# Three landing slots of three cells, transposed tiles in halves, and a stripe's left cells loaded ahead of its far cells

## The reference

```python
h = jnp.maximum(_layernorm(x, axis=-1), 0.0)
A_hat = adj + jnp.eye(adj.shape[0], dtype=adj.dtype)
d_inv_sqrt = jnp.sum(A_hat, axis=1) ** (-0.5)
A_norm = d_inv_sqrt[:, None] * A_hat * d_inv_sqrt[None, :]
support = h @ W.T
return x + jax.nn.relu(A_norm @ support)
```

## Time and profile before

| | us |
|---|---|
| median of 3 runs | 1440.7 |
| lowest, highest | 1440.1, 1442.88 |
| the profiled execution | 1437.75 |
| its span, first to last instruction | 1436.0 |

### The profile page before, as it was taken

One profiled execution on the slowest core, in us unless ns is written; L12 is line 12 of the kernel. 1 busy time (PEld: TensorE's weight loads), 2 busy tenths in 40 slices (PEclk: granted clock), 3 DMA queues, 4 the chain that ended last, 5 costly groups with the idle time before them and its releaser, 6 DMA issues.

```text
span 1436.0 us, 8302 instructions
## 1 busy us (share of the span) xinstructions
PE 1020.2 (71%) x2363; PEld 458.5 (32%) x2363; DVE 810.7 (56%) x692; ACT 511.0 (36%) x1390; POOL 52.6 (4%) x61
## 2 busy tenths in 40 slices
PE   1441354566867758759598889798899799889673
PEld 1430122222323323324243334333344234334231
DVE  5342235265656557667578677676666356556342
ACT  2685566456447354262524162524000000000001
POOL 4000000000000000000000000000000100000001
PEclk9765586787988889889899989999999899999886
DMA  9869999999998989899677796969799999898952
GB/s 308 278 250 340 322 343 324 333 310 345 341 310 264 354 222 283 262 248 297 206 248 190 221 277 179 284 184 256 212 265 272 252 272 260 266 269 219 262 118 59
DMA packets 253885, 377.07 MB, mean 263 GB/s; under 512 B 10000, under 2 KB 178064, under 8 KB 253840
## 3 DMA queue, kind: packets, MB, share of 16 engines
q1 hardware_dynamic: 136208, 192.50, 46.5%
q10 hardware_dynamic: 117632, 184.04, 41.9%
HBM read 372.31 MB, written 4.19 MB: 262 GB/s over the span
## 4 chain that ended last, share of the span: by engine, by line
DMA 36%; PE 28%; DVE 13%; ACT 11%; ACTq 4%; SPq 3%; issue 3%; POOL 0%; POOLq 0%; DVEq 0%
DMA slot<-in_adj_dram 36%; PE bank L441 27%; DVE adjT L631 9%; ACT slot L485 8%; DVE part L619 3%; ACT junk L496 3%; ACTq L289 2%; ACTq L252 1%; SPq L300 1%; SPq L307 1%; ACT acc L471 1%; SPq L315 1%; DMA out_dram<-near 1%; SPq L252 0%; ACTq L260 0%
## 5 line engine op out<-in xcount | busy, mean ns | idle before, releaser
L441 PE MATMUL bank<-adjT,support 128*128 128x512 f32 x2048 | 974.6, 636 | 309.6 <-DVE adjT L631 309.4
L631 DVE STREAM_TRANSPOSE adjT<-slot 128x2048 f32<-128x2048 f32 x211 | 483.6, 2303 | 410.4 <-DMA slot<-in_adj_dram 276.5
L441 PEld LDWEIGHTS bank<-adjT,support 128*128 128x128 f32 x2048 | 411.2, 205 | 851.6 <-issue 489.4
L496 ACT ACTIVATE junk<-slot 128x384 bf16<-128x384 f32 (+3 forms) x396 | 214.9, 544 | 307.2 <-issue 195.6
L485 ACT ACTIVATE slot<-slot 128x6656 f32<-128x6656 f32 (+12 forms) x52 | 165.4, 3183 | 90.7 <-issue 51.0
L514 ACT ACTIVATE near<-near,dinv 128x128 f32<-128x128 f32 x64 | 20.5, 390 | 408.3 <-DVE near L714 408.3
L496 ACT ACTIVATE junk<-near 128x256 bf16<-128x256 f32 (+1 forms) x176 | 69.3, 394 | 79.2 <-issue 72.4
L631 DVE STREAM_TRANSPOSE adjT<-near 128x2048 f32<-128x2048 f32 x31 | 71.2, 2300 | 38.7 <-PE bank L441 38.7
L619 DVE TENSOR_REDUCE part<-slot 128x5 f32<-128x1920 f32 (+3 forms) x36 | 84.0, 2334 | 0.0
L496 ACT ACTIVATION_READ_ACCUMULATOR junk<-slot 128x1 f32 x396 | 74.0, 187 | 0.0
L376 POOL TENSOR_TENSOR dinv<-total,power 128x4 f32<-128x4 f32 x16 | 16.1, 1008 | 895.8 <-DVE total L675 895.8
(11 more groups left out here) (53 smaller groups left out, 182.7 us busy)
## 6 DMA issues: line engine op xcount, KB each, us to landing
slot<-in_adj_dram SPq DMA_DIRECT2D x58, 1024.0 KB, 12.6
slot<-in_adj_dram ACTq DMA_DIRECT2D x58, 1024.0 KB, 15.6
slot<-in_adj_dram SPq DMA_DIRECT2D x66, 768.0 KB, 11.2
slot<-in_adj_dram ACTq DMA_DIRECT2D x66, 768.0 KB, 12.0
near<-in_adj_dram SPq DMA_DIRECT2D x30, 512.0 KB, 15.5
near<-in_adj_dram ACTq DMA_DIRECT2D x30, 512.0 KB, 16.7
third<-in_adj_dram SPq DMA_DIRECT2D x28, 256.0 KB, 15.6
third<-in_adj_dram ACTq DMA_DIRECT2D x28, 256.0 KB, 14.9
```

Of the source, the lines that this page charges most:

```text
L441: ins = nc.tensor.matmul(bank[g % BANKS][:], support[:, v * R + r, :], adjT[n % TURNS][:, r, :], start=(n == first_of[g] and r == 0), stop ...
L496: nc.scalar.activation(junk[at % JUNKS][:, :n], cells[:, c, :], ACT.Copy, accum_out=part[u % 2][:, k, c:c + 1]).then_inc(junk_done, 1)
L631: nc.vector.transpose(adjT[n % TURNS][:].rearrange("p t (c i) -> p t c i", i=Q), cells.rearrange("p c (t r) -> p t c r", r=Q)).then_inc(t_ ...
```

## The change

The numbers: slots of 3 cells, three of them (72 KB a partition in place of 64); `adjT` is a tile of half a cell, three of them (12 KB in place of 16); a cell is transposed in two instructions of 1024 elements, and its product waits for each half by itself. In the second pass the three `third` tiles, one tensor now, are a fourth slot, free once column 15 has been transposed. Small tensors of the start (stats, w_sb, wT, ones_at and others) move into `acc`, whose rows are unused by then. Pieces: 118 in place of 96 (45 left in place of 36, 38 far in place of 32, 35 again in place of 28), and 432 DMAs of them in place of 360. Of left and again pieces 53 have three cells, 25 two and two one; before 27 had four, 31 three, four two and two one.

Order: a stripe's left pieces are loaded first, then far, then near and third. `FIRST` left cells go ahead of the column in every stripe. ACT still issues two landings ahead (`AHEAD = 2`), but each now waits for the landing three before it. SP's list has the same waits and no other bound. Stripe 0 has 13 far cells, more than the 12 that a slot holds in its far form, so it gets a fifth piece of one cell's width, a second column set in `far_sum`, and one addition on VectorE. In the second pass the stores and ACT's relu stand by a rule of places: ahead of the load whose slot's former piece is transposed later than the result is combined.

```diff
-    MOST = 4
-    SLOTS = 2
-    TURNS = 2
+    MOST = 3
+    SLOTS = 3
+    AHEAD = 2
+    HALVES = 2
+    TURNS = 3
...
     for u in range(NB):
-        cells = NB - 1 - u - BAND
-        far[u] = []
-        per = 0 if cells <= 0 else min(B, MOST * C // (B * cells))
-        for b0 in range(0, B if per else 0, per or 1):
-            far[u].append(len(landing))
-            landing.append(("far", u, b0, min(per, B - b0), cells))
         left[u] = []
         for v, n in split(0, u):
             left[u].append(len(landing))
-            landing.append(("left", u, v, n, 0))
+            landing.append(("left", u, v, n, 0, 0))
+        cells = NB - 1 - u - BAND
+        far[u] = []
+        widths = [] if cells <= 0 else [cells] if cells <= MOST * B else [MOST * B, cells - MOST * B]
+        for k, width in enumerate(widths):
+            per = min(B, MOST * B // width)
+            for bb in range(0, B, per):
+                far[u].append(len(landing))
+                landing.append(("far", u, bb, min(per, B - bb), NB - cells + k * MOST * B, width))
...
+    slot_of = [m % SLOTS for m in range(AGAIN)]
+    slot_of += [((AGAIN + k % (SLOTS + 1)) % SLOTS if k % (SLOTS + 1) < SLOTS else SLOTS) for k in range(len(landing) - AGAIN)]
...
-        before = 0 if NB - 1 - s - BAND > 4 else min(FIRST, max(0, s - 1))
+        before = min(FIRST, max(0, s - 1))
...
-            if m >= SLOTS:
-                kind, u, v, n, _ = landing[m - SLOTS]
-                if kind == "again":
-                    queue.wait_ge(t_done, place[u, v + n - 1] + 1)
-                else:
-                    queue.wait_ge(act_freed, by_act[m - SLOTS])
-                if kind == "left":
-                    queue.wait_ge(dve_freed, by_dve[m - SLOTS])
+            before = before_in_slot[m]
+            if before is None:
+                if slot_of[m] == SLOTS:
+                    queue.wait_ge(t_done, transposed(column_at[NB - 1] + BAND))
+            elif landing[before][0] == "again":
+                kind, u, v, n = landing[before][:4]
+                queue.wait_ge(t_done, transposed(place[u, v + n - 1]))
+            else:
+                queue.wait_ge(act_freed, by_act[before])
+                if landing[before][0] == "left":
+                    queue.wait_ge(dve_freed, by_dve[before])
...
-        last_piece = {(far[u] + left[u])[-1]: u for u in range(NB)}
+        last_piece = {(left[u] + far[u])[-1]: u for u in range(NB)}
...
+            for m in range(AGAIN, len(landing)):
+                before = before_in_slot[m]
+                if before is not None and landing[before][0] == "again":
+                    kind, u, v, n = landing[before][:4]
+                    while stored < NB and combined_at(stored) + 1 < place[u, v + n - 1]:
+                        store(stored)
+                        stored += 1
+                load_piece(sp, (0, 1), m)
...
-                pe.wait_ge(t_done, n + 1)
...
+                for k in range(HALVES):
+                    at = HALVES * n + k
+                    pe.wait_ge(t_done, at + 1)
+                    for r in range(R // HALVES):
+                        t = k * R // HALVES + r
+                        ins = nc.tensor.matmul(bank[g % BANKS][:], support[:, v * R + t, :], adjT[at % TURNS][:, r, :],
+                                               start=(n == first_of[g] and t == 0), stop=(n == last_of[g] and t == R - 1))
+                    ins.then_inc(used, 1)
...
-                load_piece(act, (2, 3), m + SLOTS)
+                load_piece(act, (2, 3), m + AHEAD)
```

More of the change, by code:

```diff
@@ L97, in gnn_kernel @@
             again[u].append(len(landing))
[L98 to L103, removed]
+            landing.append(("again", u, v, n, 0, 0))
+    slot_of = [m % SLOTS for m in range(AGAIN)]
+    slot_of += [((AGAIN + k % (SLOTS + 1)) % SLOTS if k % (SLOTS + 1) < SLOTS else SLOTS) for k in range(len(landing) - AGAIN)]
+    before_in_slot, landed = [], []
+    for m in range(len(landing)):
+        earlier = [k for k in range(m) if slot_of[k] == slot_of[m]]
+        before_in_slot.append(earlier[-1] if earlier else None)
+        landed.append(16 * sum(2 * landing[k][3] if landing[k][0] == "far" else B for k in earlier + [m]))
     by_act = [sum(landing[k][0] != "again" for k in range(m + 1)) for m in range(len(landing))]
@@ L189, in gnn_kernel @@
         dinv = sb("dinv", [P, NT])
[L190 to L195, removed]
+        stats = acc[:, 4, :NT * 6].rearrange("p (t s) -> p t s", s=6)
+        mean, gap, var, rstd, shift = (acc[:, 5, i * NT:(i + 1) * NT] for i in range(5))
+        w_sb, wT, ones_at = (acc[:, 6, i * P:(i + 1) * P] for i in range(3))
         h = [acc[:, i, :].rearrange("p (r d) -> p r d", d=D) for i in range(2)]
@@ L280, in load_kept @@
             if u >= 2:
-                queue.wait_ge(t_done, place[u - 2, u - 1] + 1)
+                queue.wait_ge(t_done, transposed(place[u - 2, u - 1]))
             for b in quarters:
@@ L520, in _ @@
                                   x_v[b, :, q * TX:(q + 1) * TX, :]).then_inc(ld_x[q], 16)
-            for m in range(SLOTS):
+            for m in range(AHEAD):
                 load_piece(act, (2, 3), m)
@@ L532, in _ @@
                             far_sums(far[0][b // 4])
-                else:
-                    for m in far[s]:
+                    for m in far[0][NB // 4:]:
                         far_sums(m)
@@ L538, in _ @@
                     summed += 1
+                if s > 0:
+                    for m in far[s]:
+                        far_sums(m)
                 act.wait_ge(ld_near[s % 2], 16 * B * (s // 2 + 1))
@@ L546, in _ @@
             rectified = 0
-            for m in range(again[0][0] + SLOTS, len(landing)):
-                kind, u, v, n, _ = landing[m - SLOTS]
-                while rectified < NB and combined_at(rectified) < place[u, v + n - 1]:
-                    relu(rectified)
-                    rectified += 1
+            for m in range(AGAIN + AHEAD, len(landing)):
+                before = before_in_slot[m]
+                if before is not None and landing[before][0] == "again":
+                    kind, u, v, n = landing[before][:4]
+                    while rectified < NB and combined_at(rectified) < place[u, v + n - 1]:
+                        relu(rectified)
+                        rectified += 1
                 load_piece(act, (2, 3), m)
```

102 lines of the change are left out of this document (49 added, 53 removed).

## The result

The changed kernel takes 1370.8 us, the median of 4 runs (1360.35 to 1388.37), against 1440.4 (1438.76 to 1442.88) beside it: ratio 0.949, interval 0.943 to 0.955. Forecast were 1320 (1285 to 1395). Timed again beside the first experiments it took 1353.3 (1347.13 to 1373.81), ratio 0.936, interval 0.9325 to 0.9396. The rows shown are of the longest of these four, with a span of 1372.1 us. Medians are over all executions, ratios and intervals leave out those over 1.5% above a kernel's fastest, and both profiles of the changed kernel are of such an execution, so that what they show is trusted here only where another kernel shows it too. The changed kernel's times lie 27 us apart here, those of the kernel before 4 us in the first group and 11 in the second.

A forecast was written before the change was run, and what follows sets the result against it. Transfers bound the wide part; later, loads waiting for slots and TensorE waiting for transposes formed a ring. Start and wide 460, middle 478 and second pass 377 gave 1315 us of span, 1320 as median; range 1285 to 1395.

The forecast's parts named there:

- the ring: Middle and second pass: TensorE waits for VectorE's transposes, loads wait for VectorE to free slots; SP's wait 355.3 us in middle.
- The text's own case: Whole kernel: third slot and smaller pieces shorten middle and second pass; 1320 us, range 1285 to 1355, chance 0.60.
- rival 1: Middle and second pass: smaller transfers bind at 275 GB/s; 1382 us, 1387 as a median; chance 0.25.
- it costs nothing as long as these cover it: Wide part: row sums fold some 10 us later, but near's load is queued behind some 40 us of far transfers.
- The text's own other end: Wide part: if far transfers don't cover near's wait for the column, about 10 us a stripe, 60 in all.
- the start: Before the first row sums: ACT's near load leaves at 75.24, behind a fifth piece and small sums; about +5 us.
- the term of 50.7 us for the 16 cells of a stripe: Middle part, stripes 8 to 11: transfers take the wide part's time per stripe, four stripes at 51 are 204 us.
- the second pass: TensorE 341 us, 14 us to the end, 22 us of stalls: 377 us in place of 434.4, -57 us.
- waits on slots down by more than half in the middle: Sign to look for: SP's and ACT's waits for slots in the middle part fall by more than half.
- The rule on transfers: Skill's rule: spreading DMAs over queues doesn't help bandwidth; 201 GB/s would then come from 1.5 KB rows, not a lone queue.
- Rival 3: Middle and second pass: SP and ACT queues drift apart, each running alone at 201 GB/s; 1480 us, chance 0.05.
- Rivals 2 and 4: 2: VectorE binds, stripes 12 to 15 some 8 us more each, 1350 us; 4: nothing moves, 1440 us, chance 0.05.

The follow-up runs named there:

- the first experiments: Follow-up runs timed beside the kernel before, beginning with the changed kernel again, unaltered: 1353.3 us, ratio 0.936.
- far first: Changed kernel with far pieces loaded ahead of left pieces and the column first up to stripe 8, as before the change: 1311.6 us, ratio 0.9015.
- halves alone: Kernel before the change, two slots of four cells kept, with only the transposes split into halves (three half tiles): 1426.5 us, ratio 0.990.

## Why the prediction was right, and where it failed

**Right: the sign and the ring; the range in part by luck.** The text's own case ended at 1355 us. The range went on to 1395 for rival 1, and 1370.8 lies in that upper part, though rival 1 is wrong as a cause: what filled it is the wide part. The third slot does what the text said. Two slots for three in the same kernel cost 104 us by the medians (117 by the ratios), 73 of them in the middle part by the profiles. TensorE from stripe 12 on is at 94% (233.81 of 248.62) with the clock at 0.97, against 87% and 0.94 (242.52 of 278.30) before; the forecast asked for above 85%. The last L381 is at 982.88 and not near 940; 33 of these 43 us are from the start and the wide part, the others from the middle. With far first it is at 927.56.

**Wrong: "it costs nothing as long as these cover it".** The step looked at the wait that near has for the column, and found 40 us of far transfers ahead of near. It did not ask who waits for the slot that the left piece itself holds. That is the far piece three landings on, and cover for it is not 40 us but the two pieces between. The second left piece of stripe 4 can be freed only when VectorE has done the fold and the whole column, so everything behind stands. The text's own other end, "about 10 us a stripe, 60 in all", comes near in size, +52 us, and 68 against the same kernel with far first. That is luck: it was priced for near's wait behind the column, not for a slot that is held. With this term the start and wide part came to 493 us, 33 over the forecast's 460 and at its far end of +40 (492).

**Wrong: the start.** +5 us forecast, -11 measured. The step took it that ACT's load of near would leave where the next issue was, at 75.24. It left at 56.53:

```profile
31.73 5.33 ACT L496 ACTIVATE slot<-slot 128x6144 f32<-128x6144 f32 x1 [8.25 <-DMA slot<-in_adj_dram]
31.74 0.37 ACTq L258 DMA_DIRECT2D slot<-in_adj_dram  x1
...
56.53 2.42 ACTq L289 DMA_DIRECT2D near<-in_adj_dram  x2
```

With three slots and two landings ahead, ACT's load waits for a sum that ended a piece ago, and is issued at the moment in which the next sum begins. The text left that out in stripe 0. This says why the start lost nothing. Most of what it gained is a stall of ACT in front of its work on x, 10.65 us before (first line) and 2.87 after:

```profile
62.35 4.73 ACT L471 ACTIVATE acc<-support,shift,rstd 128x128 f32<-128x128 f32 x12 [10.65 <-issue]
...
64.22 4.72 ACT L482 ACTIVATE acc<-support,acc 128x128 f32<-128x128 f32 x12 [2.87 <-issue]
```

Both stalls stand behind ACT's issues of near and `third`. The start ended at 96.1 us with halves alone, at 91.3 with pieces of three in two slots and at 86.4 with the third slot, so pieces and slot share the gain. Why the issues took less time is not shown.

**Right in kind, short in size: the middle part.** 489.6 us for 478. Stripes 12 to 15 took 248.6 us, where 254 were counted (230 + 4 + 20). Stripes 8 to 11 took 241.0 for 224 (204 + 20). There the term of 50.7 us for the 16 cells of a stripe was mis-sized: that is the rate of the wide part, 329 GB/s, whose far pieces go to all partitions and in longer rows. Stripes 8 to 11 had 285 GB/s, near rival 1's 275 from stripe 9.

**Right in kind, short in size: the second pass.** 389.1 us, and 400.7 in the first profile, for 377. The far-first kernel took 367.4. What sets it between 367 and 401 in kernels with the same code there is not settled; with the stores off SP's list it was 356 to 358 in three profiles.

**Wrong: waits on slots down by more than half in the middle.** 355.3 became 332.4 with 60 us gained. It is a queue's wait, and what it costs depends on what else is on the way.

**Halves.** 1.15 to 1.24 us forecast; it is the upper end, and a sum is what it was the earlier trace rows:

```profile
L649 DVE STREAM_TRANSPOSE adjT<-slot 128x1024 f32<-128x1024 f32 x380 | 461.6, 1233 | 195.3 <-DMA slot<-in_adj_dram 103.6 <-PE bank L452 90.6
...
L634 DVE TENSOR_REDUCE part<-slot 128x5 f32<-128x1920 f32 x31 | 65.5, 2112 | 0.0
```

**Rivals.** Rival 1 came near in time (1387) and is wrong as a cause: the rate of left and again pieces comes from the partitions that they are written to, or from the columns of adj that go with these. The row's size alone doesn't make the low rate (1 KB at 347 and at 213 GB/s), nor does that of a DMA (192 KB at 353). The rule on transfers that the text set beside the rows doesn't hold for pieces of one quarter: with all loads of adj on one queue the same kernel takes 1607 us for 1312. Rival 3's mechanism exists, one queue alone is slow in such pieces, but by the count in steps of 1 us the time of it in the middle grew only from 120 to 136 us (if any packet counts, it fell from 91 to 51), and in the second pass, up to the last load of adj, it fell from 144 to 82. Rivals 2 and 4 did not come.

## What to carry to other kernels

When loads change their order, ask of each piece how long it holds its slot, from landing to its last reader, and put pieces that are held long as far behind as their readers allow: a piece that lands early but is read late takes a slot from all that follow. How much that costs depends on what follows: with several far pieces behind, in the wide part, it was 53 us, and from stripe 9 on the same order cost nothing (496 us of middle part against 502). Read a queue's waits together with whether anything is on its way in that time. Keep waits for results out of the list that issues loads, and where pieces fill part of the partitions, let the transfers that run side by side write different parts.

## What the hardware showed

A load into 32 partitions moved 201 to 213 GB/s on a single queue, and 217 with two queues in the same 32. Two queues in different halves of the partitions moved 353 (rows of 1.5 KB) to 374 (2 KB), and one queue into all 128 moved 347 (1 KB). In each of these the DMA engines' share of busy time read 1.05 or more, so it can't tell the slow case from the fast one; the GB/s beside it does. The size of a row has an effect too: both queues on far pieces with rows of 4.5 KB moved over 400, in the first slices of stripe 4 above. A load straight into all four quarters would test whether one queue suffices for the left pieces; it wasn't tried.
